# A bias added on the tensor engine, a second x2 buffer and new order lists in a three-stage post-norm decoder layer

## The chip, the cores and the metric

One core of a Trainium2 chip runs the whole kernel. The metric is the device time of one execution in microseconds (us). The engines are named as the profile names them: PE (TensorE matmul), PEld (its weight loads), DVE (VectorE), ACT (ScalarE), POOL (GpSimd) and SP (SyncE, which here only issues transfers).

## The reference

For each of 32 batches of 256 tokens with 512 channels, three blocks follow each other, each with a residual and a layer norm without weights behind it:

```python
x = _layernorm(x + _L0_attn_ref(x, Wqkv, Wout))          # stage a
x = _layernorm(x + _L0_xattn_ref(x, ctx_1024, ctx_1024, ...))  # stage b
x = _layernorm(x + _L0_ffn_ref(x, Wq, bq, ..., Wo, bo))  # stage c
```

Stage a is causal self-attention with 16 heads of 32 and rotary positions. Stage b is an mLSTM in its parallel form: 4 heads of 128 channels, gates from x and the context, a decay matrix `exp(log_d - m)`, and at its end `h * rsqrt(mean(h**2) + 1e-6) * (1.0 + rms_scale)`. Stage c routes each batch to 4 of 16 heads of 64 channels by a softmax over the mean of `x @ Wr + br`, runs attention with those heads alone, and returns `out @ Wo + bo`.

## The kernel before

**Turns.** The kernel is a software pipeline by hand. Turn s works on stage a of batch s, stage b of batch s-1 and stage c of batch s-2. There are 34 turns; 30 of them hold all three stages, the first two lack c or b and c, the last two lack a or a and b. Each engine runs one program, and each stage is a generator per engine whose `yield`s cut it into pieces. `ORDER` has one string of letters per engine; `in_turns` walks through it and runs the next piece of the stage that the letter names. So within a turn every engine's queue is fixed by its string, and an instruction that waits holds up all that stands behind it. `BANKS` says which of four PSUM banks (`ps_g`, 128x512 each) a product goes to; a bank is written again only after DVE or ACT has emptied it (the semaphores `bank_emptied_by_dve` and `bank_emptied_by_act`). The scores of stage a have a PSUM area of their own, `ps_s`.

**Precision.** Large products are taken in three f32r products of high and low parts (`mm3`), so ACT rounds each operand into a high part and DVE subtracts it to get the low part (`x_t_hi`, `x_t_lo`).

**The end of a turn.** Stage a ends with the products with `wout` (PE), the residual add into `x_tok` (DVE, L1275), layer norm statistics (DVE, L1182 and L1187), the power -1/2 on POOL (`rstd`, L1547), and the scaling into `x1` (DVE, L1288). The next turn begins with transposes through PE of x, of the context, of x1 and of x2. The first product with `wqkv` needs the low part of the new x (DVE, L1195).

**The edited parts of stage b.** After the `h` products ACT copies them into `h_raw` and squares them into `ctx_t`; DVE reduces, POOL takes a power (L1589), and DVE makes the factor `h_fac` (L1363). Then POOL scales h by the factor (L1594, two operations of 128x512), DVE multiplies by the weight `rms_w` (L1368) and adds the residual (L1370), takes statistics, and scales into `x2` (L1382).

**The edited parts of stage c.** POOL adds the bias row `bo_s`, spread over 128 partitions, to x2 (L1608, two operations of 128x512), and DVE adds the product with `wo` to that (L1507) into `y_c`, which is the same tensor. `x2` is written again only when this add on POOL is done. ACT applies the last norm and issues the store.

The instruction names in the rows drop buffer numbers: `x` stands for `x1` or `x2`, `x_t` also for `x2_t`, `ctx` for `ctx1`.

## Time and profile before

| | us |
|---|---|
| median of 3 runs | 2596.67 |
| lowest, highest | 2593.72, 2596.82 |
| the profiled execution, its own time | 2597.26 |
| its span, first to last instruction | 2595.5 |
| PE busy | 2319.3 (89%) |
| DVE busy | 1915.3 (74%) |
| ACT busy | 1425.7 (55%) |
| POOL busy | 702.2 (27%) |

The span is what the trace covers; 1.8 us of the execution lie outside it. The engines work at the same time, so their shares do not add up to one. A matmul's end is modelled and its record overlaps the next one, so busy time of PE is more than the time in which it issues.

### The profile page before, as it was taken

The numbers are of one execution on the slowest core, as the hardware profiler recorded it, in microseconds if no ns is written. First come the engines' busy times: TensorE is split into PE (matmuls) and PEld (weight loads), VectorE is DVE, ScalarE is ACT, GpSimd is POOL, SyncE is SP. The second block draws the span as 40 slices with busy tenths as digits, with TensorE's granted clock in tenths as the row PEclk, the third lists the DMA queues.
The fourth block names the chain that finished last, engine by engine and source line by source line (L and its number), as shares of the span: only waits on it lengthen the run. The fifth ranks groups of instructions, "written<-read, shape, count | busy, mean of one in ns | idle before, by whom it ended". The sixth has DMA issues, their size and how long they took to land.

```text
span 2595.5 us, 52697 instructions
## 1 busy us (share of the span) xinstructions
PE 2319.3 (89%) x19200; PEld 1861.6 (72%) x19200; DVE 1915.3 (74%) x4590; ACT 1425.7 (55%) x4586; POOL 702.2 (27%) x1065
## 2 busy tenths in 40 slices
PE   3879999999999999999999999999999999999964
PEld 3657777777777777777777777777777777777753
DVE  3568777777777777877777777777787877777753
ACT  3445655565655556565556565555656555656532
POOL 0123232222233222223222223322222332222321
PEclk9999999999999999999999999999999999999976
DMA  4010111111111111011111111111101111111111
GB/s 111 17 33 26 42 42 50 50 42 31 44 34 50 50 50 42 26 42 42 50 50 42 33 42 34 50 50 50 42 26 42 42 50 50 43 34 32 34 33 41
DMA packets 267461, 109.70 MB, mean 42 GB/s; under 512 B 215234, under 2 KB 248258, under 8 KB 267202
## 3 DMA queue, kind: packets, MB, share of 16 engines
q1 hardware_dynamic: 258498, 89.54, 14.0%
q10 hardware_dynamic: 8704, 16.78, 1.7%
q8 instruction: 153, 2.51, 0.4%
q14 instruction: 106, 0.87, 0.1%
HBM read 89.51 MB, written 16.78 MB: 41 GB/s over the span
## 4 chain that ended last, share of the span: by engine, by line
PE 50%; DVE 29%; issue 9%; ACT 7%; POOL 3%; SPq 1%; DMA 1%; POOLq 0%; DVEq 0%; ACTq 0%
PE ps_g L581 37%; PE ps_g L589 8%; PE ps_s L581 5%; ACT p_a L931 4%; DVE neg_max L1219 3%; DVE decay L1339 2%; DVE qk L1212 2%; DVE ctx_t L1370 2%; DVE x_tok L1275 2%; POOL qk_rot L1557 2%; DVE ctx_t L1368 2%; DVE ln_stat_b L1182 1%; DVE ln_stat_a L1182 1%; DVE f_max L1450 1%; DVE r_dist L1407 1%
## 5 line engine op out<-in xcount | busy, mean ns | idle before, releaser
L931 ACT ACTIVATE p_a<-ps_s,neg_max 128x128 f32<-128x128 f32 (+1 forms) x1024 | 414.6, 438 | 64.0 <-DVE neg_max L1219 64.0
L581 PE MATMUL ps_g<-x_t_hi,wqkv_hi 128*128 128x256 f32 x1024 | 305.5, 298 | 22.9 <-DVE p_t L1248 21.5
L581 PE MATMUL ps_g<-x_t_lo,wqkv_hi 128*128 128x256 f32 x1024 | 287.3, 281 | 0.0
L581 PE MATMUL ps_g<-x_t_hi,wqkv_lo 128*128 128x256 f32 x1024 | 287.1, 280 | 0.0
L1219 DVE TENSOR_REDUCE neg_max<-ps_s 128x2 f32<-128x256 f32 (+1 forms) x512 | 258.7, 546 | 7.9 <-PE ps_s L581 7.9
L1644 POOL TENSOR_SCALAR p_all<-p_all,f_rec,g_bc 128x256 f32<-128x256 f32 x256 | 152.3, 607 | 367.5 <-DVE f_rec L1458 367.5
L1557 POOL TENSOR_TENSOR qk_rot<-qk_rot,const 128x512 f32<-128x512 f32 x128 | 164.4, 1284 | 298.3 <-DVE qk_rot L1205 298.3
L982 ACT COPY p_t<-ps_g 128x384 f32<-128x384 f32 x256 | 122.0, 478 | 199.8 <-PE ps_g L589 195.5
L931 ACT ACTIVATION_READ_ACCUMULATOR p_a<-ps_s,neg_max 128x1 f32 x1024 | 230.3, 225 | 0.0
L581 PEld LDWEIGHTS ps_g<-x_t_hi,wqkv_hi 128*128 128x128 f32 x1024 | 195.7, 191 | 40.0 <-DVE p_t L1248 27.6
L589 PE MATMUL ps_g<-const,p_a 128*128 128x128 f32 x1536 | 216.4, 278 | 5.5 <-DVE att_s L1265 2.3
L589 PEld LDWEIGHTS ps_g<-const,p_a 128*128 128x128 f32 x1536 | 172.6, 142 | 41.3 <-ACT p_t L982 12.4
L581 PEld LDWEIGHTS ps_g<-x_t_lo,wqkv_hi 128*128 128x128 f32 x1024 | 196.1, 192 | 0.0
L581 PEld LDWEIGHTS ps_g<-x_t_hi,wqkv_lo 128*128 128x128 f32 x1024 | 195.2, 191 | 0.0
L931 ACT ACTIVATE p_all<-ps_g,f_bias,g_bc 128x256 f32<-128x256 f32 x256 | 141.4, 559 | 55.1 <-DVE f_bias L1453 53.2
L581 PE MATMUL ps_g<-x_t_hi,w_sel_hi 128*128 128x256 f32 x512 | 147.1, 287 | 7.2 <-DVE w_sel_lo L1431 7.2
L1265 DVE TENSOR_TENSOR att_s<-ps_g,r_bc 128x256 f32<-128x256 f32 x128 | 54.3, 424 | 131.2 <-ACT r_bc L1004 128.7
L581 PE MATMUL ps_s<-qk 32*128 32x128 f32 (+1 forms) x2048 | 121.9, 352 | 25.7 <-ACT p_a L931 22.3
L581 PE MATMUL ps_g<-x_t_lo,w_sel_hi 128*128 128x256 f32 x512 | 144.6, 282 | 0.0
L581 PE MATMUL ps_g<-x_t_hi,w_sel_lo 128*128 128x256 f32 x512 | 144.2, 282 | 0.0
L1248 DVE COPY p_t<-ps_g 128x384 f32<-128x384 f32 x256 | 136.0, 541 | 3.6 <-PE ps_g L589 0.6
L1212 DVE TENSOR_TENSOR qk<-qk,qk_rot 128x512 f32<-128x512 f32 x128 | 124.1, 970 | 17.9 <-POOL qk_rot L1557 17.9
(203 smaller groups left out, 6299.5 us busy)
## 6 DMA issues: line engine op xcount, KB each, us to landing
x_tok<-in_x SPq DMA_DIRECT2D x32, 512.0 KB, 3.7
ctx<-in_ctx SPq DMA_DIRECT2D x64, 256.0 KB, 3.4
p_all<-in_L_ffn_Wq SPq DMA_DIRECT2D x128, 128.0 KB, 2.7
pt_all<-in_L_ffn_Wk SPq DMA_DIRECT2D x128, 128.0 KB, 3.0
y_out<-in_L_ffn_Wv SPq DMA_DIRECT2D x128, 128.0 KB, 3.2
out<-y_out ACTq DMA_DIRECT2D x32, 512.0 KB, 2.8
...
```

The costliest lines, as they stand in the source:

```text
L581: return nc.tensor.matmul(o, l, r, start=first, stop=last)
L589: return nc.tensor.transpose(o, i, ident)
L931: return nc.scalar.activation(o, i, f, **kw)
L982: nc.scalar.copy(p_t[:, 2 * p % 4, :], bank[("turn", 2 * p), b][:, 0:CAUSAL]).then_inc(act_emptied.sem)
L1182: v.bn_stats(ln[which][0][:, t, :], y[:, t, :]).then_inc(ln_stats[which].sem)
L1212: v.tensor_tensor(qk[:, 2 * u:2 * u + 2, :], qk[:, 2 * u:2 * u + 2, :], qk_rot, ALU.add).then_inc(roped.sem)
L1219: m = v.tensor_reduce(neg_max[i][:, :, t], ps_s[:, 2 * i:2 * i + 2, t * P:t * P + P * (t + 1)], AX.X, ALU.max, negate=True)
L1248: v.tensor_copy(p_t[:, (2 * p + 1) % 4, :], bank[("turn", 2 * p + 1), b][:, 0:CAUSAL]).then_inc(dve_emptied.sem)
L1265: v.tensor_tensor(att_s, bank[("att", u), b][:, 0:T], r_bc, ALU.mult).then_inc(dve_emptied.sem)
L1275: v.tensor_tensor(y_a[b % 2][:, t, :], bank[("out", t), b], x_tok[b % 2][:, t, :], ALU.add).then_inc(dve_emptied.sem)
L1557: g.tensor_tensor(qk_rot, qk_rot, c["sin"].unsqueeze(1).to_broadcast([P, 2, T]), ALU.mult).then_inc(sin_scaled.sem)
L1644: n = g.tensor_scalar(p_f[k % 2][:, t, :], p_f[k % 2][:, t, :], f_rec[:, k, t:t + 1], g_bc[:, k:k + 1], ALU.mult, ALU.mult)
```

## The change

It has four parts.

**The FFN's output bias.** POOL's two adds of `bo_s` go. The bias is held as a high and a low row (rows 0 and 32 of a 33-row f32r tensor of zeros otherwise), and PE adds it with one product of K=33 and 512 columns ahead of each of the two `wo` products; it waits for the bank alone, and the wait for the attention output now stands behind it.

**x2 in two buffers.** The sum with `wo` is now written over x2 itself, and `x2[b % 2]` alternates. DVE's scaling into x2 no longer waits for POOL's add but for ACT's last norm of two batches earlier.

**h scaled and weighted at once.** POOL's two operations on h and DVE's two multiplies by `rms_w` go; eight DVE operations of 128x128, one per head and half, do `(h_raw * h_fac) * rms_w`.

**Lists of turns and banks.** All five strings of `ORDER` and the table `BANKS` are new. No other instruction is added or taken away in a turn. Ahead of the first turn DVE has three more small operations (a column of ones, the high and the low bias row) and POOL one (zeros in the 33 rows), and all engines wait for them.

```diff
 ORDER = {
     "tensor": (
-        "acbcbbaacabbabbbaccabbacabcbbaaaabbaababcababcbcbcbbabbaabbbcbbbbbcabbbbbbabbbaccacccacaaacaacccaacacbaaacaaaa"
+        "bbabaaccbcbaaaaacaaabaaaaaaaaaaaabcbbaaabbaaaaaaaaaaaabaaaaaccbabcacbabcacaaaacaacaaaaaacabaaccacacccbccbbbacb"
...
-    bo_s = sb("bo_s", [P, D])
+    bo_parts = sb("bo_parts", [LO_AT + 1, D], F32R)
+    one_r = sb("one_r", [LO_AT + 1, 1], F32R)
...
-    x2 = sb("x2", [P, TT, D])
+    x2 = [sb(f"x2_{i}", [P, TT, D]) for i in range(2)]
...
-    x2_bo = sb("x2_bo", [P, TT, D])
-    y_c = x2_bo
+    y_c = x2
...
             for t in range(TT):
                 o = bank[("wo", t), b]
+                pe.wait_ge(*freed[("wo", t), b])
+                mm(o, one_r.to_broadcast([LO_AT + 1, P]), bo_parts, True, False)
                 pe.wait_ge(*empty[("fatt", 1), b])
-                pe.wait_ge(*freed[("wo", t), b])
                 for k in range(2):
-                    done = mm3(o, part(att_f, slice(None), k, slice(t * P, (t + 1) * P)), part(wo_s, slice(None), k), k == 0, k == 1)
+                    done = mm3(o, part(att_f, slice(None), k, slice(t * P, (t + 1) * P)), part(wo_s, slice(None), k), False, k == 1)
...
-                dve.wait_ge(*h_scaled(b, t + 1))
-                v.tensor_tensor(h_sq[:, t], h_sq[:, t], rms_w.unsqueeze(1).to_broadcast([P, HX, DX]), ALU.mult).then_inc(h_weighted.sem)
+                dve.wait_ge(*fac_made(b))
+                for h in range(HX):
+                    w = v.scalar_tensor_tensor(h_sq[:, t, h], h_raw[:, t, h, 0:DX], h_fac[:, t, h:h + 1], rms_w, ALU.mult, ALU.mult)
+                w.then_inc(h_weighted.sem)
...
-                dve.wait_ge(*with_bo(b - 1))
-            for t in range(TT):
-                m = v.tensor_scalar(x2[:, t, :], y_b[:, t, :], ln["b"][1][:, t, 0:1], ln["b"][2][:, t, 0:1], ALU.subtract, ALU.mult)
+            if b > 1:
+                dve.wait_ge(*y_made(b - 2))
+            for t in range(TT):
+                m = v.tensor_scalar(x2[b % 2][:, t, :], y_b[:, t, :], ln["b"][1][:, t, 0:1], ln["b"][2][:, t, 0:1], ALU.subtract, ALU.mult)
...
-                dve.wait_ge(*with_bo(b, t + 1))
                 dve.wait_ge(*full[("wo", t), b])
-                v.tensor_tensor(y_c[:, t, :], bank[("wo", t), b], x2_bo[:, t, :], ALU.add).then_inc(dve_emptied.sem)
+                v.tensor_tensor(y_c[b % 2][:, t, :], bank[("wo", t), b], x2[b % 2][:, t, :], ALU.add).then_inc(dve_emptied.sem)
...
-            pool.wait_ge(*fac_made(b))
-            for t in range(TT):
-                g.tensor_tensor(h_sq[:, t], h_raw[:, t, :, 0:DX], h_fac[:, t].unsqueeze(2).to_broadcast([P, HX, DX]), ALU.mult).then_inc(h_scaled.sem)
...
-            pool.wait_ge(*x2_made(b))
-            if b:
-                pool.wait_ge(*y_made(b - 1))
-            for t in range(TT):
-                g.tensor_tensor(x2_bo[:, t, :], x2[:, t, :], bo_s, ALU.add).then_inc(with_bo.sem)
```

**Where instructions stand now.** PE's queue at the boundary of two full turns, before: the end of stage a's output products lies just ahead of it, then come the transposes of x (`x_tok`), of x2 and x1 (`x`) and of the context (`ctx`).

```order
L589 MATMUL ps_g<-const,x_tok 128x128 [waits bank_emptied_by_dve,x_loaded1]
L589 MATMUL ps_g<-const,x_tok 128x128 x3
L589 MATMUL ps_g<-const,x 128x128 [waits x2_made]
L589 MATMUL ps_g<-const,x 128x128 x3
L589 MATMUL ps_g<-const,ctx 128x128 [waits bank_emptied_by_dve,ctx_loaded]
L589 MATMUL ps_g<-const,ctx 128x128 x3
L589 MATMUL ps_g<-const,ctx 128x128 [waits bank_emptied_by_act]
L589 MATMUL ps_g<-const,ctx 128x128 x3
L589 MATMUL ps_g<-const,x_tok 128x128 [waits bank_emptied_by_act]
L589 MATMUL ps_g<-const,x_tok 128x128 x3
L589 MATMUL ps_g<-const,x 128x128 x4
L589 MATMUL ps_g<-const,x 128x128 [waits bank_emptied_by_dve,x1_made]
```

After the change, the same place, from the last `wout` product on:

```order
L582 MATMUL ps_g<-wout_hi,x_t_lo 128x512
L590 MATMUL ps_g<-const,ctx 128x128 [waits bank_emptied_by_dve,ctx_loaded]
L590 MATMUL ps_g<-const,ctx 128x128 x3
L590 MATMUL ps_g<-const,x_tok 128x128 [waits x_loaded1]
L590 MATMUL ps_g<-const,x_tok 128x128 x3
L590 MATMUL ps_g<-const,ctx 128x128 x4
L590 MATMUL ps_g<-const,x_tok 128x128 x4
L590 MATMUL ps_g<-const,x_1 128x128 [waits bank_emptied_by_act,x2_made]
L590 MATMUL ps_g<-const,x_1 128x128 x3
L590 MATMUL ps_g<-const,x_1 128x128 [waits bank_emptied_by_act]
L590 MATMUL ps_g<-const,x_1 128x128 x3
L590 MATMUL ps_g<-const,x 128x128 [waits bank_emptied_by_dve,x1_made]
```

The first transposes of the context come ahead of those of x, and wait for the bank that DVE's second residual add empties; x2 (here `x_1`) comes behind the context and x.

DVE's queue at the end of a turn, before, from the first add of the `wo` product (L1507) to stage a's residual adds (L1275):

```order
L1507 TENSOR_TENSOR x_bo<-ps_g,x_bo 128x512 [waits bank_filled]
L1265 TENSOR_TENSOR att_s<-ps_g,r_bc 128x256 [waits att_lo,r_spread]
L1507 TENSOR_TENSOR x_bo<-ps_g,x_bo 128x512 [waits bank_filled]
L1269 TENSOR_TENSOR x_t_lo<-att_s,x_t_hi 128x256 [waits att_hi]
L1236 RECIPROCAL p_rec<-p_sum 128x8 [waits r_widened,exped]
L1248 COPY p_t<-ps_g 128x384 [waits bank_filled] x2
L1182 BN_STATS ln_stat_c<-x_bo 128x6 [waits bank_emptied_by_dve] x2
L1187 BN_AGGR ln_mv_c<-ln_stat_c 128x2 [waits ln_stats_c] x2
L1265 TENSOR_TENSOR att_s<-ps_g,r_bc 128x256 [waits att_lo,r_spread]
L1517 SCALAR_TENSOR_TENSOR ln_shift_c<-ln_mv_c,ln_rstd_c 128x2 [waits ln_aggr_c,ln_rstd_c]
L1269 TENSOR_TENSOR x_t_lo<-att_s,x_t_hi 128x256 [waits att_hi]
L1275 TENSOR_TENSOR x_tok<-ps_g,x_tok 128x512 [waits bank_filled] x2
```

After the change, from the last residual add of stage b (L1374) to stage a's residual adds (L1277); `x_1` and `x_0` are the two x2 buffers:

```order
L1374 TENSOR_TENSOR ctx_t<-ctx_t,x 128x512 [waits h_weighted]
L1184 BN_STATS ln_stat_b<-ctx_t 128x6 [waits y_b_made] x2
L1189 BN_AGGR ln_mv_b<-ln_stat_b 128x2 [waits ln_stats_b] x2
L1511 TENSOR_TENSOR x_1<-ps_g,x_1 128x512 [waits bank_filled]
L1267 TENSOR_TENSOR att_s<-ps_g,r_bc 128x256 [waits att_lo,r_spread]
L1511 TENSOR_TENSOR x_1<-ps_g,x_1 128x512 [waits bank_filled]
L1271 TENSOR_TENSOR x_t_lo<-att_s,x_t_hi 128x256 [waits att_hi]
L1184 BN_STATS ln_stat_c<-x_1 128x6 [waits bank_emptied_by_dve] x2
L1189 BN_AGGR ln_mv_c<-ln_stat_c 128x2 [waits ln_stats_c] x2
L1387 TENSOR_SCALAR x_0<-ctx_t,ln_mv_b,ln_rstd_b 128x512 [waits y_made,ln_aggr_b,ln_rstd_b]
L1387 TENSOR_SCALAR x_0<-ctx_t,ln_mv_b,ln_rstd_b 128x512
L1277 TENSOR_TENSOR x_tok<-ps_g,x_tok 128x512 [waits bank_filled] x2
```

Stage b's end (eight scalings L1371, two adds L1374, statistics, scaling into x2 L1387), which stood in the middle of the turn, now stands at its end, between the second half of the `wo` sums and the residual adds of stage a.

PE's queue at the `h` products of stage b (`ctx,decay`), before: they follow the `c` products (`h_raw,ctx_t`) directly.

```order
L581 MATMUL ps_g<-h_raw,ctx_t 128x256 [waits bank_emptied_by_act]
L581 MATMUL ps_g<-h_raw,ctx_t 128x128
L581 MATMUL ps_g<-h_raw,ctx_t 128x256 [waits bank_emptied_by_dve]
L581 MATMUL ps_g<-h_raw,ctx_t 128x128
L581 MATMUL ps_g<-ctx,decay 128x129 [waits bank_emptied_by_dve]
L581 MATMUL ps_g<-ctx,decay 128x129
L581 MATMUL ps_g<-ctx,decay 128x129 [waits bank_emptied_by_dve]
L581 MATMUL ps_g<-ctx,decay 128x129 x9
L581 MATMUL ps_s<-qk 128x128 [waits exped,qk_roped]
L581 MATMUL ps_s<-qk 128x128 x3
L581 MATMUL ps_s<-qk 128x256 x4
```

After the change:

```order
L582 MATMUL ps_g<-pt_all,v_f 64x256 [waits bank_emptied_by_act]
L582 MATMUL ps_g<-pt_all,v_f 64x256 x3
L582 MATMUL ps_g<-ctx,decay 128x129 [waits bank_emptied_by_act]
L582 MATMUL ps_g<-ctx,decay 128x129
L582 MATMUL ps_g<-ctx,decay 128x129 [waits bank_emptied_by_dve]
L582 MATMUL ps_g<-ctx,decay 128x129
L582 MATMUL ps_g<-ctx,decay 128x129 [waits bank_emptied_by_dve]
L582 MATMUL ps_g<-ctx,decay 128x129 x3
L582 MATMUL ps_g<-ctx,decay 128x129 [waits bank_emptied_by_act]
L582 MATMUL ps_g<-ctx,decay 128x129 x3
L590 MATMUL ps_g<-const,p_all 128x128 [waits bank_emptied_by_act,f_normed]
```

The `h` products have moved behind stage c's first attention product (`pt_all,v_f`), late in the turn, and each waits for a bank that ACT or DVE empties.

## Rows read from the trace of the kernel before

**Rows 1.** Windows (us, busy PE, PEld, DVE, ACT, POOL, clock): full turn, last two.

```profile
1314.13:1390.79 76.66, 71.34 (x605) 57.33 (x608) 59.41 (x143) 44.24 (x143) 21.95 (x34) 1.00 0.17 42
...
2467.00:2531.90 64.90, 44.58 (x254) 34.06 (x253) 34.86 (x83) 20.57 (x54) 15.17 (x27) 0.71 0.14 33
2531.90:2595.50 63.60, 28.34 (x159) 22.18 (x157) 21.65 (x54) 15.32 (x35) 9.81 (x20) 0.68 0.16 42
```

**Rows 2.** The page: the chain that ended last, by engine.

```profile
PE 50%; DVE 29%; issue 9%; ACT 7%; POOL 3%; SPq 1%; DMA 1%; POOLq 0%; DVEq 0%; ACTq 0%
```

**Rows 3.** Timeline (start, us, what, [idle before <-releaser]): PE, from turn to turn.

```profile
1318.17 0.40 PE L581 MATMUL ps_g<-wout_hi,x_t_lo 128*128 128x512 f32 x1
1318.41 0.60 PE L589 MATMUL ps_g<-const,x_tok 128*128 128x128 f32 x4
...
1323.60 0.63 PE L589 MATMUL ps_g<-const,x 128*128 128x128 f32 x4 [0.36 <-DVE x_t_lo L1195]
1324.20 0.39 PE L581 MATMUL ps_g<-x_t_hi,wqkv_hi 128*128 128x256 f32 x1
```

**Rows 4.** Timeline of DVE over the same start.

```profile
1317.91 1.39 DVE L1275 TENSOR_TENSOR x_tok<-ps_g,x_tok 128x512 f32<-128x512 f32 x2 [1.20 <-PE ps_g L581]
1319.22 1.27 DVE L1182 BATCH_NORM_STATS2 ln_stat_a<-x_tok 128x6 f32<-128x512 f32 x2
1320.41 0.30 DVE L1187 BATCH_NORM_AGGREGATE ln_mv_a<-ln_stat_a 128x2 f32<-128x6 f32 x2
1321.85 1.00 DVE L1288 TENSOR_SCALAR x<-x_tok,ln_mv_a,ln_rstd_a 128x512 f32<-128x512 f32 x2 [1.14 <-POOL ln_rstd_a L1547]
1322.77 1.38 DVE L1195 TENSOR_TENSOR x_t_lo<-ps_g,x_t_hi 128x512 fp32r<-128x512 f32 x2
```

**Rows 5.** Timeline of PE: waits in the rest of the same turn.

```profile
1334.76 0.80 PE L581 MATMUL ps_g<-log_f,const 128*128 128x4 f32 x6 [0.62 <-ACT v_a L946]
...
1364.95 0.39 PE L581 MATMUL ps_g<-x_t_hi,wqkv_hi 128*128 128x256 f32 x1 [0.57 <-DVE p_t L1248]
...
1375.30 0.63 PE L589 MATMUL ps_g<-const,p_all 128*128 128x128 f32 x4 [0.66 <-ACT p_t L982]
...
1378.83 0.94 PE L581 MATMUL ps_s<-qk 32*128 32x128 f32 x16 [0.70 <-ACT p_a L931]
```

**Rows 6.** Timeline of POOL in the same turn.

```profile
1328.62 1.28 POOL L1557 TENSOR_TENSOR qk_rot<-qk_rot,const 128x512 f32<-128x512 f32 x1 [6.80 <-DVE qk_rot L1205]
1329.85 2.98 POOL L1608 TENSOR_TENSOR x_bo<-x,bo_s 128x512 f32<-128x512 f32 x2
...
1353.39 1.66 POOL L1589 TENSOR_TENSOR h_ssq<-h_ssq,minus_half 128x8 f32<-128x8 f32 x1 [7.01 <-DVE h_ssq L1360]
1355.33 2.04 POOL L1594 TENSOR_TENSOR ctx_t<-h_raw,h_fac 128x512 f32<-128x512 f32 x2 [0.28 <-DVE h_fac L1363]
```

**Rows 7.** Timeline of DVE around the first rotary product and the router.

```profile
1327.79 0.74 DVE L1205 STREAM_SHUFFLE qk_rot<-ps_g 128x512 f32<-128x512 f32 x1
...
1329.93 1.76 DVE L1212 TENSOR_TENSOR qk<-qk,qk_rot 128x512 f32<-128x512 f32 x1 [0.38 <-POOL qk_rot L1557]
...
1331.79 1.07 DVE L1407 TENSOR_SCALAR r_dist<-r_e,r_s 1x16 f32<-1x16 f32 x1
```

**Rows 8.** Groups by line and form (count | busy, mean ns | idle): DVE, one turn.

```profile
L1339 DVE SCALAR_TENSOR_TENSOR decay<-ps_g,decay 128x384 f32<-128x384 f32 x4 | 1.9, 545 | 0.0
...
L1265 DVE TENSOR_TENSOR att_s<-ps_g,r_bc 128x256 f32<-128x256 f32 x4 | 1.7, 424 | 3.9 <-ACT r_bc L1004 3.8
...
L1370 DVE TENSOR_TENSOR ctx_t<-ctx_t,x 128x512 f32<-128x512 f32 x2 | 1.4, 692 | 0.1
...
L1368 DVE TENSOR_TENSOR ctx_t<-ctx_t,rms_w 128x512 f32<-128x512 f32 x2 | 1.4, 682 | 0.0
```

**Rows 9.** Timeline of ACT behind the products of stage b.

```profile
1349.34 0.37 ACT L1061 COPY h_raw<-ps_g 128x258 f32<-128x258 f32 x1 [0.52 <-PE ps_g L581]
1349.75 1.15 ACT L931 ACTIVATE ctx_t<-h_raw 128x512 f32<-128x512 f32 x2
```

More of the change, by code:

```diff
@@ L57 @@
+        "caccaacc"
     ),
@@ L230, in build @@
     squared, ssq_step, ssq_powed, fac_made = count("h_squared", TT), count("ssq_step", TT + 3), count("ssq_powed"), count("fac_made")
-    h_scaled, h_weighted, y_b_made = (count(n, TT) for n in ("h_scaled", "h_weighted", "y_b_made"))
-    x2_hi, with_bo = count("x2_hi", TT), count("with_bo", TT)
+    h_weighted, y_b_made = (count(n, TT) for n in ("h_weighted", "y_b_made"))
+    x2_hi = count("x2_hi", TT)
     routed, r_exped, top_exped, b_picked = count("route_step", 11), count("r_exped"), count("top_exped"), count("b_picked", KF)
@@ L809, in stage_c @@
             pe.wait_ge(*x2_made(b))
-            yield from transposed(b, "x2", x2)
+            yield from transposed(b, "x2", x2[b % 2])
             o = bank[("logit",), b]
@@ L1156, in stage_c @@
             for t in range(TT):
-                A(y_out[:, t, :], y_c[:, t, :], ACT.Identity, scale=rs[:, t, 0:1], bias=shift[:, t, 0:1]).then_inc(y_made.sem)
+                A(y_out[:, t, :], y_c[b % 2][:, t, :], ACT.Identity, scale=rs[:, t, 0:1], bias=shift[:, t, 0:1]).then_inc(y_made.sem)
             act.wait_ge(*y_made(b))
@@ L1169, in scalar @@
         act.wait_ge(setup_loaded.sem, SETUP)
-        act.wait_ge(tables_ready.sem, 5)
-        act.wait_ge(half_ready.sem, 5)
+        act.wait_ge(tables_ready.sem, 8)
+        act.wait_ge(half_ready.sem, 6)
         act.wait_ge(stage_split.sem, PIECES)
```

52 lines of the change are left out of this document (29 added, 23 removed), and 8 rows, old and new, of the table BANKS.

## The prediction, made before the changed kernel ran

> **What bounds the kernel now.** I read the windows first, then the chain, then the timelines of one turn. A full turn takes 76.66 us, and there are 30 of them; the last two turns, which lack stage a, take 64.9 and 63.6 us at a granted clock of about 0.7 [rows 1]. So the full turn decides. In it PE has records for 71.34 us and is idle for 5.32, DVE is busy for 59.41, ACT for 44.24 and POOL for 21.95 [rows 1]. The chain that ended last is half PE and 29% DVE [rows 2]. The reader is to see that PE comes close to its limit and still loses time in hand-offs, and that POOL is no bound at all.
>
> How much does PE lose? A matmul of 512 columns has a record of 0.40 us, but the next one starts 0.24 later [rows 3], so behind each wait some 0.17 us of a modelled end hide further lost time. With 5.3 us recorded and about 14 waits of that kind, PE loses 5.3 + 2.4 = 7.7, and issues for 76.66 - 7.7 = 69.0 us. These waits fall in two parts.
>
> The first is the turn's start. From the first transpose of x (1318.41) to the first product with `wqkv` (1324.20) pass 5.79 us, in which PE has seven groups of four transposes (a record of 0.60 each, of which the same 0.17 overlaps, so some 0.44), or 3.1 us; 2.7 are lost [rows 3]. The cause is DVE's chain of stage a's norm: residual adds from 1317.91, statistics, POOL's power, scaling, low part ending at 1324.15, so 6.29 us from the first add to PE's product [rows 3, 4]. The second part is 5.0 us in the rest of the turn, in a dozen hand-offs, of which the largest are recorded with 0.57 to 0.70 us: DVE's and ACT's copies out of the banks and the exponentials ahead of the next scores [rows 5].
>
> **The change part by part.**
>
> *The bias on PE.* Two products of 512 columns per turn, at the 0.24 us from start to start of such a product [rows 3]: +0.5 us of PE per turn. They stand ahead of the wait for the attention output, and could fill an idle slot, but by the rows of the order there is other work just ahead, so I charge them fully: bounds 0 and 0.8 (at the record's 0.40 each).
>
> *POOL's adds gone.* 2.98 us per turn of POOL [rows 6]. Nobody waits for POOL there. But they held DVE: beside them the rotary add took 1.76 us, against 0.69 for other operations of its size, and a 16-element operation of the router took 1.07 [rows 7, 8]. 2.0 us of DVE come back. Neither was what PE waited for: PE's next scores had to wait for the product ahead of them. In the new order they shorten the same chain, which now is in the way (below). The Trainium skill ("SBUF — State Buffer", "SBUF: two separate sides") says that VectorE and GpSimd take their shared ports as an exclusive lock for a whole instruction; the stretched operations above agree with it.
>
> *h scaled and weighted on DVE.* Gone are POOL's 2.04 us [rows 6] and two DVE operations of 0.68 [rows 8]. New are eight of 128x128. No row has that size. Four operations of the same kind with 384 columns have a busy time of 1.9 us with a record of 0.545 each [rows 8], so they start (1.9 - 0.545) / 3 = 0.46 apart; 384 columns at the 0.96 columns per ns that the step from 256 (0.424) to 512 columns (0.692) gives [rows 8] are 0.40, which leaves 0.06 per operation. With 128 columns that is 0.13 + 0.06 = 0.2 us, 1.6 for eight. Bounds: 1.1 (eight times the pure columns) and 3.4 (eight records of 0.42, the smallest form of comparable kind in the rows). I take 1.6, since these operations are independent of each other as the four were.
>
> *The new lists.* Here is most of the sum. I follow the new queue from the first `wqkv` product (R = 0) through the same durations as in the turn before.
>
> First stretch, R to the end of the `h` products. PE's issue there is the turn's 69.0 + 0.5 less what the order now puts behind it: four groups of three transposes (1.4), two of `p_all` (0.9), one attention product of stage c (1.0), eighteen and six products with `wout` (4.1 + 1.4), two `wo` sums with bias (3.2), one attention product of stage a (1.2), and the seven groups of the turn's start (3.1): 69.5 - 16.3 = 53.2. Waits in it: the scores of the first four heads need the rotary chain, which from the shuffle to its add takes 2.14 + 0.7 [rows 7], 3.1 with the hand-offs; the 512-column products put in front of them take 2.85, so 0.2 is lost. The scores of the second four heads need the same chain, with only 1.9 us of transposes, logits and gate products in front: 1.2 lost. Behind these, nine smaller ones where a product waits for its bank's copy (0.05 to 0.35 each): 1.2. Together 2.6, so the `h` products end at 55.8.
>
> Second stretch, a chain through DVE. Now stage b's end stands last in the turn. ACT's copy and two squares 0.2 + 0.37 + 1.15 [rows 9]; DVE's two reductions and three small operations 2.0; POOL's power 1.66 [rows 6]; the factor 0.2; eight scalings 1.6; two adds 1.4 (0.69 each [rows 8]); statistics 1.6 [rows 4]; then, in DVE's queue, the two `wo` sums with stage a's last attention piece between them and behind, 1.9; statistics again 1.5; scaling into x2 1.0 (as its twin for x1 [rows 4]); only then the residual adds. Sum 14.6: the first residual add starts at 70.4. PE's last `wout` product would be done at 55.8 + 13.2 + 0.7 of waits = 69.7, so DVE is last by some 0.7.
>
> Third stretch: 6.29 us from that add to the next R, as before, since statistics, POOL's power and both scalings are the same [rows 4]. The context's transposes wait for the second residual add, but the chain is longer than what PE has left, so it costs nothing more.
>
> The new turn is 70.4 + 6.3 = 76.7 by this count, against 76.66. In the same count I rounded each hand-off up; by single durations the three stretches give 55.4, 14.45 and 6.3, or 76.15. I take 76.4, near the middle: **-0.25 us per full turn, -7.5 for 30.**
>
> *Outside the full turns.* The setup has three more DVE operations that wait for each other, and all engines wait: +1.5 (bounds 0.5 and 3). In the turn without stage a the `c` and `h` products, which stood in the wait for the selected weights, now stand between pieces of stage c's attention while the clock is low [rows 1]; +2 (bounds -2 and +5). x2's second buffer is worth nothing in a full turn: in the trace no row waits for POOL's add.
>
> **Sum.** From the profiled execution's 2597.26 (0.6 above the median of the runs): 2597.3 - 7.5 + 1.5 + 2 = 2593; less the 2 to 3 us by which the shorter end of stage b (1.6 + 1.4 against 2.04 + 2.8 on two engines) should help in the turns with few stages: **2591**. Of a full turn I know 0.2% only as 0.17 us; 0.2% (5 us) is also what a measurement can tell from no change.
>
> **The rivals.**
>
> 1. *DVE's tail is longer (slower).* The second stretch has no slack: each microsecond more in DVE's last twenty operations is a microsecond per turn. It decides from +0.4 us on. Before, stage b's end stood in the middle of DVE's turn, with other work of PE beside it; that cover is gone. If the eight scalings take 0.33 apart instead of 0.2 (+1.0), or the hand-offs of the first stretch lose 1 us more than I count (before they lost 5.0 where I count 3.3), the turn is 77.4: 2597.3 + 0.75 x 30 + 1 = 2621. For it: DVE's 29% of the chain and the sum 76.7 above. Against it: operations of the same kind follow each other with 0.06 us of extra time. Chance 28%.
>
> 2. *A fixed price for each small operation (slower).* If each scaling paid its fixed part fully, eight would take 8 x 0.3 = 2.4 us, 0.8 more per turn, and the end would be 2591 + 24 = 2615. The 0.3 is the 0.424 of 256 columns less 128 columns. The Trainium skill ("VectorE: DVE Perf Modes", "The TRN2 errata — SBUF-src ops pay a fixed extra latency per instruction") states such a rule: many small tiles pay the latency per tile, and 512 elements or more are advised. The trace speaks against it for operations that do not depend on each other (0.46 apart at 384 columns). Chance 8%.
>
> 3. *More of the waits go (faster than I say).* The new lists might leave PE with the tail as its only wait, since the bank waits of the first stretch are short; with 1.2 of them and half of the tail's excess gone, the turn is 75.2: 2597.3 - 44 + 1 = 2554, or up to 2575 with less of it. For it: 7.7 us of lost time are there to be won, and DVE has 2.0 + 1.1 us less to do. Against it: the norm's chain at the start is untouched. Chance 14%.
>
> 4. *Nothing that can be measured.* The turn is within 0.15 us of 76.66: 2592 to 2602. The two counts above enclose it. Chance 16%.
>
> **How the numbers follow.** The forecast (2575 to 2592, turn 75.9 to 76.5) has 34%; with rival 3 that gives 0.48 for faster; rival 4 gives 0.16; rivals 1 and 2 give 0.36 for slower. The range must hold rival 1's 2621 and the upper half of rival 3: 2562 to 2621, with about 1 in 10 beyond each end. The likeliest case alone has 2575 to 2592.
>
> **What would show it.** The first residual add (now L1277) should follow the turn's last scaling into x2 (L1387) at once, with no idle time before it for PE: if it waits for PE, DVE's tail is shorter than I say. The scalings L1371 should have a record near 0.29 us and start 0.2 apart. The rotary add should take 0.69 everywhere, and the router's operation 0.15. PE should wait before the second scores of stage a for over 0.5 us, and about 3.6 us in all at the turn's start. The forecast is wrong if full turns are not 76.2 to 76.6: below, through fewer bank waits than nine; above, through DVE's tail or a bank's copy that stands behind a late operation in ACT's or DVE's queue.

## The result, and the profile after

The changed kernel takes 2609.2 us (median of 4 runs, 2608.05 to 2612.79) against 2595.19 for the kernel before on the same chip (4 runs, 2592.21 to 2596.82): ratio 1.0055, 95% interval 1.0042 to 1.0068. It is slower by 0.55%. I had forecast 2591, so the sign was wrong. The profiled execution took 2608.05, with a span of 2606.3. This and the runs below were taken on several chips, on which the kernel before took 2595.2 to 2596.8, so times of two different runs can be compared to some 2 us.

A turn is measured here from one start of the scaling into `x1` (L1290 after, L1288 before) to the next. The first window is one of the shortest full turns, the second the longest, the third all that follows the last such mark; columns as in [rows 1].

```profile
553.34:630.09 76.75, 71.75 (x602) 58.74 (x602) 58.65 (x150) 44.22 (x145) 17.17 (x29) 1.00 0.17 42
1247.48:1325.77 78.29, 72.12 (x602) 58.63 (x602) 58.52 (x150) 44.20 (x145) 17.16 (x29) 1.00 0.16 42
2483.68:2606.30 122.62, 75.78 (x402) 57.20 (x402) 52.27 (x137) 35.19 (x88) 17.39 (x39) 0.64 0.16 39
```

Before, the 30 full turns were all 76.6 to 76.7 us (one of them stands in [rows 1]). After, they lie between 76.74 and 78.29 while every engine does the same work in them: that is the first thing to see, because nothing in the forecast varies from turn to turn. The chain that ended last, to be read beside [rows 2]:

```profile
PE 46%; DVE 21%; issue 14%; ACT 8%; SPq 4%; POOL 4%; DMA 3%; ACTq 0%; DVEq 0%; POOLq 0%
```

SP's queue and the transfers now hold 7% of the chain, where they had 2%. PE's 50% has become 46, DVE's 29% has become 21. So what is new on the path is no engine that I had counted. The waits of ACT (engine, line, what it waited for: us in total, times, longest) name it:

```profile
ACT w_sel_hi L1093 <- DMA p_all<-in_L_ffn_Wq: 30.5, 31, 6.0
ACT w_sel_hi L1093 <- DMA y_out<-in_L_ffn_Wv: 23.8, 32, 2.4
ACT w_sel_hi L1093 <- DMA pt_all<-in_L_ffn_Wk: 17.2, 20, 1.8
```

The same waits in the kernel before:

```profile
ACT w_sel_hi L1091 <- DMA y_out<-in_L_ffn_Wv: 17.4, 23, 1.3
ACT w_sel_hi L1091 <- DMA p_all<-in_L_ffn_Wq: 6.3, 1, 6.3
ACT w_sel_hi L1091 <- DMA pt_all<-in_L_ffn_Wk: 1.7, 1, 1.7
```

So ACT waited there too, in most turns for the third load (0 to 1.3 us), and yet the full turns had one length; for the first two loads it waited in the last turn alone. L1093 is ACT's cast of the FFN weights that the router selected. These weights are loaded in every turn, after the router's pick is known. The timeline of DVE, SP's queue and ACT in the short turn above (its mark is 553.34), then ACT in the long one (its mark is 1247.48):

```profile
573.70 0.16 DVE L1416 FIND_INDEX8 r_idx<-r_dtop,r_dist 1x8 uint32<-1x16 f32 x1
576.25 2.05 SPq L558 DMA_DIRECT2D p_all<-in_L_ffn_Wq  x4
...
580.59 2.11 SPq L558 DMA_DIRECT2D y_out<-in_L_ffn_Wv  x4
580.74 1.04 ACT L1093 CAST w_sel_hi<-p_all 128x1024 fp32r<-128x1024 f32 x1 [0.25 <-DMA p_all<-in_L_ffn_Wq]
...
585.59 1.05 ACT L1093 CAST w_sel_hi<-y_out 128x1024 fp32r<-128x1024 f32 x1 [0.32 <-DMA y_out<-in_L_ffn_Wv]
...
1281.83 1.05 ACT L1093 CAST w_sel_hi<-y_out 128x1024 fp32r<-128x1024 f32 x1 [2.41 <-DMA y_out<-in_L_ffn_Wv]
1282.79 0.47 ACT L984 COPY p_t<-ps_g 128x384 f32<-128x384 f32 x1
```

The pick stands 20.4 us behind the mark. SP issues the first of twelve transfers 2.5 us later and the last of them 6.0 us behind the first (6.0 to 7.4 over all turns), and the last weights are cast 32.25 us behind the mark in the short turn, 34.35 in the long turn, where ACT waits 2.41 us for them. Over the 30 full turns this last cast starts 32.3 to 34.4 us behind the mark. Behind the cast in ACT's queue stands a copy of `p_t` that PE needs. Before, the pick stood at 11.3 us (1333.17 against the mark 1321.85), and the same casts at 21.0, 21.9 and 23.5, of which in this turn one waited for 0.31 (the last one starts at 23.0 to 24.5 over the full turns):

```profile
1333.17 0.16 DVE L1411 FIND_INDEX8 r_idx<-r_dtop,r_dist 1x8 uint32<-1x16 f32 x1
...
1342.84 1.16 ACT L1091 CAST w_sel_hi<-p_all 128x1024 fp32r<-128x1024 f32 x1
...
1345.35 1.04 ACT L1091 CAST w_sel_hi<-y_out 128x1024 fp32r<-128x1024 f32 x1 [0.31 <-DMA y_out<-in_L_ffn_Wv]
```

The end of a short turn on DVE, which answers to [rows 4] and to what the forecast called the second stretch:

```profile
616.68 0.17 DVE L1365 TENSOR_TENSOR h_fac<-h_ssq,h_den 128x8 f32<-128x8 f32 x1
616.88 1.14 DVE L1371 SCALAR_TENSOR_TENSOR ctx_t<-h_raw,h_fac,rms_w 128x128 f32<-128x128 f32 x4
618.06 0.69 DVE L1374 TENSOR_TENSOR ctx_t<-ctx_t,x 128x512 f32<-128x512 f32 x1
618.67 1.13 DVE L1371 SCALAR_TENSOR_TENSOR ctx_t<-h_raw,h_fac,rms_w 128x128 f32<-128x128 f32 x4
619.83 0.69 DVE L1374 TENSOR_TENSOR ctx_t<-ctx_t,x 128x512 f32<-128x512 f32 x1
...
622.89 0.69 DVE L1511 TENSOR_TENSOR x<-ps_g,x 128x512 f32<-128x512 f32 x1
...
625.26 1.00 DVE L1387 TENSOR_SCALAR x<-ctx_t,ln_mv_b,ln_rstd_b 128x512 f32<-128x512 f32 x2
626.18 1.28 DVE L1277 TENSOR_TENSOR x_tok<-ps_g,x_tok 128x512 f32<-128x512 f32 x2
...
630.09 1.01 DVE L1290 TENSOR_SCALAR x<-x_tok,ln_mv_a,ln_rstd_a 128x512 f32<-128x512 f32 x2 [1.14 <-POOL ln_rstd_a L1556]
```

The four scalings L1371 take 1.14 us with a record of 0.30 each, so they start (1.14 - 0.30) / 3 = 0.28 us apart. The residual adds (L1277) start at once behind the scaling into x2 (L1387), as forecast, at 626.18. PE over the same stretch, to be read beside [rows 3]:

```profile
625.95 0.39 PE L582 MATMUL ps_g<-wout_hi,x_t_lo 128*128 128x512 f32 x1
627.61 0.63 PE L590 MATMUL ps_g<-const,ctx 128*128 128x128 f32 x4 [1.27 <-DVE x_tok L1277]
...
630.76 0.63 PE L590 MATMUL ps_g<-const,x 128*128 128x128 f32 x4 [1.21 <-ACT ctx_t L1026]
...
632.49 0.37 PE L582 MATMUL ps_g<-x_t_hi,wqkv_hi 128*128 128x256 f32 x1
```

### The profile page after: what moved, and what is told of

It reads as the page before. It is cut to its first block, busy times and chain, and to the rows that moved or that the text cites. A ratio compares the mean times of both kernels' runs of the same rounds, so it can differ in the third digit from the quotient of the medians.

```text
span 2606.3 us, 52890 instructions
## 1 busy us (share of the span) xinstructions
PE 2337.7 (90%) x19264; PEld 1903.6 (73%) x19264; DVE 1895.4 (73%) x4785; ACT 1427.0 (55%) x4586; POOL 551.3 (21%) x938
## 4 chain that ended last, share of the span: by engine, by line
PE 46%; DVE 21%; issue 14%; ACT 8%; SPq 4%; POOL 4%; DMA 3%; ACTq 0%; DVEq 0%; POOLq 0%
PE ps_g L582 36%; PE ps_g L590 8%; POOL qk_rot L1566 3%; DVE neg_max L1221 3%; SPq L558 2%; PE ps_s L582 2%; DVE p_t L1250 2%; DMA pt_all<-in_L_ffn_Wk 2%; ACT y_out L933 2%; DVE f_max L1455 2%; DVE ln_stat_c L1184 1%; ACT ctx_t L933 1%; DVE decay L1341 1%; ACT x_t_hi L941 1%; DVE qk_rot L1207 1%
## 5 line engine op out<-in xcount | busy, mean ns | idle before, releaser
L1221 DVE TENSOR_REDUCE neg_max<-ps_s 128x2 f32<-128x256 f32 (+1 forms) x512 | 257.5, 544 | 54.2 <-PE ps_s L582 54.2
L582 PE MATMUL ps_g<-x_t_hi,wqkv_hi 128*128 128x256 f32 x1024 | 294.9, 288 | 1.4 <-DVE x_t_lo L1197 1.4
L590 PE MATMUL ps_g<-const,p_a 128*128 128x128 f32 x1536 | 222.0, 278 | 23.1 <-ACT p_t L984 11.5
L933 ACT ACTIVATION_READ_ACCUMULATOR p_a<-ps_s,neg_max 128x1 f32 x1024 | 223.1, 218 | 0.0
L1645 POOL TENSOR_SCALAR p_all<-p_all,f_rec,g_bc 128x256 f32<-128x256 f32 x256 | 143.0, 568 | 258.0 <-DVE f_rec L1463 255.1
L582 PE MATMUL ps_s<-qk 32*128 32x128 f32 (+1 forms) x2048 | 121.6, 352 | 40.3 <-DVE qk L1214 40.3
L1006 ACT COPY r_bc<-ps_g 128x256 f32<-128x256 f32 x128 | 47.8, 374 | 192.4 <-PE ps_g L582 192.2
L1214 DVE TENSOR_TENSOR qk<-qk,qk_rot 128x512 f32<-128x512 f32 x128 | 88.6, 693 | 87.9 <-POOL qk_rot L1566 87.9
L1591 POOL TENSOR_SCALAR_AFFINE_SELECT decay<-decay 128x256 f32<-128x256 f32 x128 | 49.4, 409 | 473.2 <-ACT decay L933 473.2
L1250 DVE COPY p_t<-ps_g 128x384 f32<-128x384 f32 x256 | 140.5, 549 | 12.3 <-PE ps_g L590 8.3
```

Of the source, the lines that this page charges most:

```text
L582: return nc.tensor.matmul(o, l, r, start=first, stop=last)
L590: return nc.tensor.transpose(o, i, ident)
L933: return nc.scalar.activation(o, i, f, **kw)
L1214: v.tensor_tensor(qk[:, 2 * u:2 * u + 2, :], qk[:, 2 * u:2 * u + 2, :], qk_rot, ALU.add).then_inc(roped.sem)
L1221: m = v.tensor_reduce(neg_max[i][:, :, t], ps_s[:, 2 * i:2 * i + 2, t * P:t * P + P * (t + 1)], AX.X, ALU.max, negate=True)
L1250: v.tensor_copy(p_t[:, (2 * p + 1) % 4, :], bank[("turn", 2 * p + 1), b][:, 0:CAUSAL]).then_inc(dve_emptied.sem)
```

## The experiments

Eleven kernels ran. For each I give the full turns (30 of them, mean) and the stretch behind the last mark beside the time; the same split for the two kernels themselves is: before, 172.0 us up to the first full turn, 30 x 76.65, 124.1 behind; after, 167.1, 30 x 77.22, 122.6.

**1. The edits with the old lists.** The two tables `ORDER` and `BANKS` are those of the kernel before; nothing else differs from the changed kernel.

> The changed kernel's edits (bias on PE, x2 in two buffers, h scaled and weighted by eight operations) with the lists of turns and of banks of the kernel before. Theory A (the loss lies in the new lists, which put the router's pick at 20.4 us of the turn instead of 11.3, so that the selected weights land after ACT wants them): here ACT's casts of the weights wait for no load of q or k, and full turns are of one length. Only the bias is new on PE, 0.42 us per turn where its cost is full: turn 76.7 to 77.1, time 2597 to 2611. Rival (the edits carry the loss, eight small operations and two f32r products, wherever they stand): 2609 or more. If the 2.0 us of DVE time that POOL's adds held are worth something here: below 2595.

Measured: 2616.39 us, ratio 1.0076 (1.0063 to 1.0089). This is above theory A's range and in the rival's. Full turns are 77.44 in the mean and nearly all between 77.41 and 77.45, so the variation belongs to the new lists; but the edits are not free either. The waits of PE, first of this kernel, then of the kernel before:

```profile
PE ps_g L582 <- DVE p_t L1250: 44.4, 31, 5.0
```

```profile
PE ps_g L581 <- DVE p_t L1248: 21.5, 31, 5.8
```

22.9 us more of waits for one copy of `p_t` on DVE. In DVE's queue the scalings stand ahead of it: from the start of the first to the statistics behind the last add it is 3.54 us (1366.82 to 1370.36), where the two weightings and adds took 2.65 (1357.67 to 1360.32).

**2. The lists alone.** The kernel before, with the new `ORDER` and `BANKS`.

> The kernel before with the new lists of turns and banks only. Theory A: the weights land late here too, turns vary as in the changed kernel by 0 to 1.5 us, so the lists alone are no gain, 2605 or more. Besides, POOL's scaling of h (2.04 us) and the two weightings (1.4) stand in the tail now in place of eight operations of 0.28 (2.3), so the tail gains 0.4 to 1.2 us per turn, and POOL's x2 adds (3.0) may stand ahead of the power that x1 waits for: 2605 to 2660. Rival (the lists are good and the edits carry the loss): below 2596.

Measured: 2658.95 us, ratio 1.0245 (1.0224 to 1.0265), full turns 78.3 to 81.1, mean 78.8. PE waits 54.2 us for the `wo` adds (DVE `x_bo`) and 72.1 for the rotary add, against 40.3 in the changed kernel and 40.8 in run 8, which has h as here but no adds of POOL: so the rest of the rotary add's 72.1 goes with POOL's adds. The new lists need the edits, and with them still lose.

**3. The weights without the router.** The routing of the weights is left out.

```diff
-            sp.wait_ge(*routed(b, 6))
...
-            picks = [engine.value_load(r_idx[0:1, k:k + 1], ...) * DF for k in range(KF)]
...
-                    engine.dma_start(w_raw[j][:, :, k, :], col(...)[:, :, bass.ds(picks[k], DF)])
+                    engine.dma_start(w_raw[j][:, :, k, :], col(...)[:, :, k * DF:(k + 1) * DF])
```

> The changed kernel, but the FFN weights of heads 0 to 3 are loaded in every turn, with no wait for the router's pick (the routing of the weights is left out; the router's operations stay). Theory A: the casts wait for no load, all full turns are 76.75 us like the shortest now, 29 x 0.45 = 13 us less: 2593 to 2598, with the variation between turns gone. Rival (the variation comes from elsewhere, as DVE's tail or the store of the output): 2606 to 2612 as now.

Measured: 2587.2 us, ratio 0.9966 (0.9953 to 0.9979). It is 22.0 us faster than the changed kernel, and faster than the kernel before. Full turns are 76.71 to 76.79 but for three (the first, and two of 77.1), mean 76.81, and the stretch behind the last mark is 113.5 instead of 122.6:

```profile
551.47:628.23 76.76, 71.79 (x602) 58.77 (x602) 58.64 (x150) 44.00 (x145) 17.16 (x29) 1.00 0.17 42
2471.07:2584.60 113.53, 70.80 (x402) 54.40 (x402) 52.08 (x137) 34.89 (x88) 17.86 (x39) 0.72 0.17 42
```

So of 21.7 us of span, 12.3 come from the full turns, 9.1 from the last two, where, without stage a, less work covers the late weights. The theory had the size of the first part (13) and had not asked for the second.

The 9.1 have two parts, and one of them is no cost of the change. From the last router's pick to the end pass 54.1 us in the changed kernel and 48.9 here, so 5.2 of the 9.1 come from the last turn; there ACT waits for the three loads 6.04, 1.75 and 1.15 us in the changed kernel, and 6.27, 1.71 and 1.03 in the kernel before, which takes 52.4 from that pick to its end. The other 3.9 come from the turn without stage a ahead of it, where ACT waits 6.2 us in the changed kernel and 0.7 in the kernel before. So what the new queue adds is some 16.5 us (12.3, 3.9 and 0.3 at the start) and not 22. The kernel before did not run with fixed weights.

**4. One scaling in place of four.** The norm's weight `rms_w` is left out.

```diff
-                for h in range(HX):
-                    w = v.scalar_tensor_tensor(h_sq[:, t, h], h_raw[:, t, h, 0:DX], h_fac[:, t, h:h + 1], rms_w, ALU.mult, ALU.mult)
+                w = v.tensor_tensor(h_sq[:, t], h_raw[:, t, :, 0:DX], h_fac[:, t].unsqueeze(2).to_broadcast([P, HX, DX]), ALU.mult)
```

> The changed kernel, but h is scaled by one DVE operation of 128x512 per half instead of four of 128x128 (the weight of the norm is left out). If the four start 0.28 us apart (1.14 for four) against 0.68 for the one, 0.9 us leave DVE's tail. Theory B (DVE's tail is the last, but PE's last wout product ends only 0.4 us earlier): 0.3 to 0.5 us per turn, 2594 to 2600. Rival 1 as predicted, every microsecond of the tail counts: 0.9 per turn, 2580 to 2584. If PE is last anyway: 2607 to 2611.

Measured: 2604.39 us, ratio 1.0029 (1.0019 to 1.0039). The shortest full turns are 76.65 to 76.77 as before this edit, though 0.9 us has left DVE's tail; the few microseconds come at the start (the second mark stands at 165.8 instead of 167.1) and from the last turns (120.7 instead of 122.6). The time lies in none of the three ranges, and both expectations on the tail fell. DVE's timeline shows where the 0.9 us went:

```profile
1001.89 0.17 DVE L1365 TENSOR_TENSOR h_fac<-h_ssq,h_den 128x8 f32<-128x8 f32 x1
1002.10 0.69 DVE L1370 TENSOR_TENSOR ctx_t<-h_raw,h_fac 128x512 f32<-128x512 f32 x1
...
1008.10 0.69 DVE L1510 TENSOR_TENSOR x<-ps_g,x 128x512 f32<-128x512 f32 x1 [0.94 <-PE ps_g L582]
...
1010.47 1.00 DVE L1386 TENSOR_SCALAR x<-ctx_t,ln_mv_b,ln_rstd_b 128x512 f32<-128x512 f32 x2
1011.38 1.28 DVE L1277 TENSOR_TENSOR x_tok<-ps_g,x_tok 128x512 f32<-128x512 f32 x2
```

DVE is early, and then waits 0.94 us for PE's second `wo` sum (L1510). From there on its queue is as before.

**5. The router's operations one place earlier.** In VectorE's string two letters for stage c move two places forward: L1402 to L1407 stand ahead of the rotary add of the second four heads.

> The changed kernel with one entry of VectorE's list moved: the router's first three operations stand ahead of the rotary add of the second four heads (in the idle 0.9 us in which that add waits for POOL) instead of behind it. The pick should come 1.1 us earlier, at 19.3 us of the turn instead of 20.4, and nothing is added to any engine. Theory A (weights land 0 to 1.5 us too late in full turns, 12 us in all, and more in the last two): most of the full turns' excess over 76.75 goes, 8 to 12 us, and 1 to 3 us at the end: 2594 to 2601. Rival (lateness is not what varies, fixed picks gained because the queue ran far from other transfers): 2606 to 2612.

Measured: 2594.47 us, ratio 0.9987 (0.9978 to 0.9996), 14.7 us faster than the changed kernel, in theory A's range. In 26 of the 30 full turns the pick is at 19.36 us instead of 20.36, so 1.0 us of the 1.1 came (in the others it is at 19.7 or later); the full turns are 76.62 to 77.5, mean 76.79, and only 13 casts of q's weights wait where 31 did. The full turns give 12.8 us; of these some 3 are no late weights, since the shortest turns are shorter as well (76.66 against 76.75). With nothing left out it supports what run 3 showed without the routing.

**6. Rotary products ahead of the values.** In `stage_a` of the planner and of every engine:

```diff
-            yield from values(1)
             yield from rotary(1)
+            yield from values(1)
...
-    "v": "31", ... "qk": "1330",
+    "v": "33", ... "qk": "1130",
```

> The changed kernel, but PE makes the rotary products of the second four heads ahead of the second half of the values instead of behind, with their two banks exchanged. The 0.90 us that PE waits for the second scores is then covered by 2.85 us of products, and the router's operations, which stand behind the rotary add in VectorE's queue, come 1 us earlier relative to PE's work. Expected if both terms are as I read them: full turns 75.9 to 76.3 us, little variation, 2568 to 2585. Rival (the time goes on waiting in the next place, since the exponentials or VectorE's maxima set the pace behind): full turns 76.6 to 76.8, only the late weights gained, 2590 to 2598.

Measured: **2557.6 us, ratio 0.9847 (0.9834 to 0.9860)**: faster than both kernels, and below my range. Full turns are 75.76 to 76.17 (the first 76.7), mean 75.86: in them 40.8 us go, of which 28.5 are 30 times 0.95 and the rest late weights. I had not counted what goes ahead of them (161.4 up to the first of them instead of 167.1) and behind (119.1 instead of 122.6). The waits of PE for the rotary add, changed kernel and this one:

```profile
PE ps_s L582 <- DVE qk L1214: 40.3, 64, 3.1
```

```profile
PE ps_s L582 <- DVE qk L1214: 10.1, 33, 0.3
```

30.2 us of wait gone, and the turn 0.95 shorter than 76.75: the wait of 0.90 us, whose place the forecast had named (with 1.2), was on the path in full. Run 11 against run 3, both without late weights, gives the same: full turns of 75.80 against 76.75. In the kernel before PE waited for this add 3.4 us in all, so the wait had come with the new lists. The casts then wait for q's weights 11 times. The exchange of banks came along with the new order and was not tried alone.

**7. The old lists, bias on PE, h as before.** Run 1, with POOL's scaling and DVE's weighting of h put back.

> The old lists, bias on PE and x2 in two buffers, but h scaled by POOL and weighted by VectorE in one operation per half as before. In the run with the old lists and all edits, full turns are 77.43 against 76.65, and PE waits 44.4 us for VectorE's copies of p_t where it waited 21.5 before: the eight operations stand ahead of such a copy. If they are all of the 0.78 us per turn, the two bias products are hidden and this is 2594 to 2600, full turns 76.6 to 76.8. If the products cost their 0.42: 2606 to 2611, 77.0 to 77.1.

Measured: 2594.04 us, ratio 0.9986 (0.9977 to 0.9995), full turns 76.55, in the first of the two ranges. The two bias products are hidden there: with POOL's adds gone and x2 in two buffers they leave the turn 0.1 us shorter. PE's wait for `p_t` is back at 20.2 us. The step from here to run 1 is the eight scalings alone: 0.89 us per turn, which is the 3.54 - 2.65 of DVE's queue.

**8. The new lists, h as before.** The changed kernel with the same part put back.

> The changed kernel, but h scaled by POOL and weighted by VectorE in one operation per half as before; the new lists, bias on PE and x2's two buffers stay. In the tail the eight operations and two adds take 3.6 us from the factor on; POOL's first scaling 1.1, VectorE's four operations and the wait for POOL's second make 3.8 to 4.1. Since PE's last product ends where VectorE's first residual add starts, each 0.1 beyond counts: full turns 76.9 to 77.3, 2612 to 2622. If the shortest turns stay at 76.75, the tail has more slack than I read; if they come near the 78.3 of the lists with the old edits, then h and not POOL's adds was what cost there.

Measured: 2639.66 us, ratio 1.0165 (1.0151 to 1.0179), above my range; shortest full turns 77.55, mean 78.1. So here the eight scalings *gain* at least 0.8 us per turn. POOL and DVE in this kernel's tail:

```profile
935.72 2.04 POOL L1601 TENSOR_TENSOR ctx_t<-h_raw,h_fac 128x512 f32<-128x512 f32 x2 [0.28 <-DVE h_fac L1365]
...
935.47 0.17 DVE L1365 TENSOR_TENSOR h_fac<-h_ssq,h_den 128x8 f32<-128x8 f32 x1
936.79 1.51 DVE L1370 TENSOR_TENSOR ctx_t<-ctx_t,rms_w 128x512 f32<-128x512 f32 x1 [1.15 <-POOL ctx_t L1601]
938.34 0.69 DVE L1372 TENSOR_TENSOR ctx_t<-ctx_t,x 128x512 f32<-128x512 f32 x1
938.95 0.68 DVE L1370 TENSOR_TENSOR ctx_t<-ctx_t,rms_w 128x512 f32<-128x512 f32 x1
939.67 0.69 DVE L1372 TENSOR_TENSOR ctx_t<-ctx_t,x 128x512 f32<-128x512 f32 x1
```

The first weighting L1370 takes 1.51 us instead of 0.68: it ends 0.54 behind the end of POOL's second scaling (937.76), nearly as if it had begun only then. From the factor to the end of the last add it is 4.9 us against 3.8 with the eight scalings. I had put it at 3.8 to 4.1, without that hold.

**9 and 10. Without the bias products; and without them and with one scaling.**

```diff
-                mm(o, one_r.to_broadcast([LO_AT + 1, P]), bo_parts, True, False)
```

> The changed kernel without the two bias products (the FFN's output bias is left out). With one scaling in place of four the shortest full turns stayed at 76.75 although 0.9 us had left VectorE's tail. Theory C: at the turn's end PE's last product and VectorE's last scaling into x2 fall together, so taking from one alone gives nothing. Then here too the shortest turns stay at 76.65 to 76.75, and only late weights may shift the time: 2604 to 2610. Rival (PE alone is last): 0.42 us per turn, shortest turns 76.3, 2594 to 2598.

> Both of these together: no bias products and one scaling in place of four (bias and the norm's weight are left out). Theory C: now both chains are shorter, PE's by 0.42 and VectorE's by 0.9, so the shortest full turns are 76.3 to 76.4, with 10 to 13 us less than with one scaling alone (2604.4): 2591 to 2595. If PE alone is last, it equals the run without bias; if neither, both stay at 76.75.

Measured: 2600.07 us (1.0016, 1.0006 to 1.0026) without the bias, between the two ranges, and 2571.64 (0.9912, 0.9895 to 0.9929) without the bias and with one scaling, far below its range. The shortest full turns are 76.5 to 76.6 and 75.7. In the mean of the full turns neither edit alone gives more than 0.2 us (77.21 in run 4 and 77.04 in run 9, against 77.22); both together take 1.04 from the shortest turns, where I had expected 0.4. PE's timeline around the two bias products, first with them (run 4, mark 938.54), then without (run 10, mark 926.36):

```profile
1002.66 0.39 PE L582 MATMUL ps_g<-wout_hi,x_t_lo 128*128 128x512 f32 x1
1002.99 0.49 PE L582 MATMUL ps_g<-bo_parts,one_r 33*128 33x512 f32 x1
1003.41 0.50 PE L582 MATMUL ps_g<-wo_hi,x_t_hi 128*128 128x512 f32 x1
1003.74 0.39 PE L582 MATMUL ps_g<-wo_lo,x_t_hi 128*128 128x512 f32 x1
...
1006.00 0.50 PE L582 MATMUL ps_g<-bo_parts,one_r 33*128 33x512 f32 x1
1006.42 0.50 PE L582 MATMUL ps_g<-wo_hi,x_t_hi 128*128 128x512 f32 x1
```

```profile
990.47 0.41 PE L582 MATMUL ps_g<-wout_hi,x_t_lo 128*128 128x512 f32 x1
990.71 0.40 PE L582 MATMUL ps_g<-wo_hi,x_t_hi 128*128 128x512 f32 x1
990.95 0.40 PE L582 MATMUL ps_g<-wo_lo,x_t_hi 128*128 128x512 f32 x1
...
993.20 0.50 PE L582 MATMUL ps_g<-wo_hi,x_t_hi 128*128 128x512 f32 x1
```

With the first bias product there are 0.75 us from the last product with `wout` to the first with `wo`, without it 0.24; and the next `wo` product then starts 0.33 behind (1003.74) instead of 0.24 (990.95). So it costs 0.60 us, not its 0.24. The second costs the 0.42 up to the product behind it, which has a record of 0.50 with the bias product and without (993.20). From the last `wout` product to the second sum's first `wo` product it is 3.76 us against 2.73: two of them make 1.03. Why they cost more than others of 512 columns is not shown. In the trace of run 4 the weight loads of the bias product and of the one behind it start together with their products (1002.99, 1003.41), where most others start one product ahead; but so does that of 993.20 in run 10, which has 128 rows.

**11. Run 6 with the weights of run 3.**

> The kernel with rotary products ahead of values, and the FFN weights of heads 0 to 3 loaded without a wait for the router (the routing of the weights is left out). It says how much of the late weights is left there: full turns are 75.80 with four of 31 at 76.1, so at most 1.5 us there, and 5 to 6 us after the last full turn, where stage a is gone and the router's pick has less work behind it: 2550 to 2553. If nothing is left: 2557.

Measured: 2547.96 us (0.9823, 0.9806 to 0.9839), 9.6 us below run 6 by the times and 6.2 by the two ratios, just below the range. Of the spans' difference of 10.3, 2.6 lie before the first full turn, 1.6 in the full turns (75.81) and 6.1 behind the last mark. Late weights still cost that much in the fastest kernel that computes everything (run 6).

## Why the prediction was wrong

**The step that failed is one that it left out: the transfers that follow the router's pick.** Under "The new lists" I followed PE, DVE, ACT and POOL through a full turn from the first `wqkv` product, but took the selected weights to be there; a wait for them is named for the turn without stage a alone. The trace of the kernel before had the price: from the pick to the cast of the last weights pass 12.2 us (1333.17 to 1345.35), with a wait for the transfer at its end. The new queue has the pick at 20.4 us and ACT's last cast where it can start 31.8 us behind the mark (run 3, 583.31 against 551.47). The difference is 11.4 us. So the last weights are late by 0.4 to 2.5 us, 1.3 in the mean; by 45 us of the long turn PE is 1.2 us behind the short one. Run 3 shows the cost, 22.0 us (each of the two times is known to some 3 us), of which some 16.5 are new with the change and the rest lies in the last turn, where the kernel before waits as long; run 5 gives back 14.7 with nothing left out.

**A second step failed beside it: the full turn itself was taken too short.** Without late weights it is 76.76 (run 3), where I took 76.4 and where the kernel before has 76.65. The count by single durations had 55.4, 14.45 and 6.3; measured are 55.5, 14.94 and 6.31, and the eight scalings alone are 0.65 longer than I had them. So the new turn has no gain over the old one, and the forecast's -7.5 us for 30 of them was never there. The balance: the full turns are 24.5 us above the forecast (30 times 77.22 against 76.4), of which 12.3 are late weights. What lies outside them is 6.3 us shorter than before, where I had it 1 longer, so 7.3 below. Together that is 17.2; the profiled execution is 17.05 above 2591.

Whether the forecast's sign would stand without late weights is open. Run 3's 2587.2 is below the kernel before, but by some 5 us for the last turn alone, in which the kernel before is charged for its own late weights; without these 5 it would be some 4 us faster. Run 5 is faster than before by 0.13% (0.04 to 0.22).

**That 2587 is near 2591 is partly luck.** Against the kernel before, run 3 gains 5.2 us ahead of the full turns and 10.5 behind the last mark, where I had +1.5 for the setup, +2 for the drain and 2 to 3 of gain in short turns: some 17 us too pessimistic, of which 5 are waits of the last turn that run 3 alone is spared. Its full turns are 0.16 us *longer* than before where I had 0.25 shorter: 12 us too optimistic.

**First stretch: right.** The `h` products end at 611.24, 55.5 us behind R = 555.74; forecast 55.4 to 55.8. PE's wait for the second scores is 0.90 (forecast over 0.5). What I did not see is what run 6 shows: that this wait was the cheapest 28 us in the kernel.

**Second stretch: the sum right, two terms small.** The first residual add starts 70.44 behind R (626.18), forecast 70.4. Since I said that I rounded up and then took 76.4 from the middle of 76.15 and 76.7, the choice was wrong: the rounding covered two undersized terms. The scalings start 0.28 apart and not 0.2 (+0.65 for eight), nearer to rival 1's 0.33 and rival 2's 0.3; and the bias products cost 1.03 and not 0.5, above my upper bound of 0.8 (PE's side of the tail; on its own this is hidden but for 0.2, run 9).

**Rival 1 had the sign and not the mechanism.** It said that each microsecond more in DVE's tail is one in the turn. Run 8 made DVE's part 1.1 longer and lost 0.8, which is near that; but run 4 took 0.9 us out and got nothing, run 9 took 1.0 us out of PE's queue and got 0.2, and run 10 took both and got 1.04. The adds of the `wo` sums are where PE and DVE meet: DVE takes the second at 622.89, 0.46 behind its operation before, where the same two stand 0.33 apart in run 8, so it had 0.13 to spare; and the 3.3 us of DVE behind that add set the end. The forecast's "PE's last product would be done at 69.7, so DVE is last by some 0.7" looked for the meeting at the last product. They meet one sum of stage c earlier.

**Rival 2, a price per small operation: it is there, and costs only where nothing else is late.** 128 columns are 0.13 us at [rows 8]' rate, the distance is 0.28, so 0.15 of fixed time per operation, not the 0.06 that I had from four operations of 384 columns. It cost 0.89 per turn with the old lists (run 1 against run 7), nothing on the short turns of the new (run 4), and 0.8 there with the bias products out of the way (run 10 against run 9). By the Trainium skill ("VectorE: DVE Perf Modes", "The TRN2 errata — SBUF-src ops pay a fixed extra latency per instruction") every tile pays; the traces agree in kind, but at 384 columns only 0.06 shows, and no run says why.

**POOL's adds gone: right.** The rotary add takes 0.69 everywhere (mean 0.693 over all, 0.97 before); run 7 shows that with the old lists this, the second x2 buffer and the bias products together give 0.1 us per turn, so it lay off the path there as forecast; with the new lists runs 2 and 8 show that the adds would have stood in the way. The router's operation takes 0.22, not 0.15. Run 8's stretched weighting beside POOL's scaling is one more case of what the Trainium skill ("SBUF — State Buffer", "SBUF: two separate sides") describes as an exclusive lock for a whole instruction; the trace agrees (1.51 us for 0.68). **x2's second buffer:** forecast as worth nothing by itself; no run tried it alone, so this is not shown. The third stretch took 6.31 (626.18 to 632.49), forecast 6.29; the waits recorded in it are 1.27, 1.21 and 0.26, 2.7 in all and not the 3.6 that I named, since part hides in modelled ends.

What stays open: why single transfers of 128 KB land after 2.1 us in one turn and 5.2 in another. They did so before as well (2.2 to 4.5, median 3.0 in both), and the turns were of one length: the change did not make them vary, it took away the slack that had hidden it. With the fixed weights of run 3 the variation between turns is gone but for three turns; no run took the single transfers apart.
